# Softmax sums of a decoder layer: the probabilities of two key tiles are added on VectorE before the round with ones, and the order is rewritten

## The chip, the core and the metric

The kernel runs on one core of one Trainium2 chip. The core has five engines that run side by side, each through its own queue in order: TensorE (matmul, PE in the profile; its weight loads are shown apart as PEld), VectorE (DVE), ScalarE (ACT), GpSimd (POOL) and SyncE (SP, which issues the DMAs). They meet only through semaphores. The metric is the device time of one launch in microseconds (us), the median of the runs.

## The reference, cut to what matters

32 sequences of 256 tokens by 256 features go through one decoder layer: layer norm and self-attention with rotary embedding (16 heads of 16 features), layer norm and cross-attention to 77 context tokens (16 heads), and then a graph of six nodes, each of them an attention with 8 heads of 32 features over its own mixes of earlier nodes, with a last layer norm. All of it is float32. The attention of a node is:

```python
q = ew[c, 0] * (nodes[in_q] @ We[eq] + be[eq])
k = ew[c, 1] * (nodes[in_k] @ We[ek] + be[ek])
v = ew[c, 2] * (nodes[in_v] @ We[ev] + be[ev])
...
scores = jnp.einsum('bqhd,bkhd->bhqk', qh, kh) / jnp.sqrt(jnp.asarray(dh, q.dtype))
attn = jax.nn.softmax(scores, axis=-1)
ctx = jnp.einsum('bhqk,bkhd->bqhd', attn, vh).reshape(B, S, d)
...
nodes[c] = act_w[c] * o + q
```

The change concerns the sum under the softmax, over 256 keys, which the kernel keeps as two key tiles of 128.

## The kernel before, in words

A launch is a prologue (weights are loaded and folded, about 128 us), one pass over the pieces marked as running ahead, and a loop of 16 iterations. An iteration carries two sequences, called slot 0 and slot 1, through eight stages: stage 0 is self-attention (SELF), stage 1 cross-attention (CROSS), stages 2 to 7 are the nodes. The slots run interleaved, so that one has matmuls while the other waits for a chain.

The work is cut into pieces, and one text, `ORDER` (lines 134 to 201), lists all pieces of an iteration. Each engine walks through this list and issues those that are its own, in this order; nothing else sets the order. A name such as `PV1.3.0@6` reads: piece PV, slot 1, stage 3, group 0, in PSUM bank 6. A plus marks a piece that works on the next iteration's sequence. What a piece must wait for is worked out from the list as counts of semaphores.

The pieces of one group of four heads (SELF and CROSS have four groups a slot, a node two) are, in order:

- S, SB on TensorE: scores, queries in rows, from a high and a low half (three products); MX on VectorE (line 863): the maximum of each row, two heads an operation; NM on GpSimd (679, 682): the negated maximum, split in two halves.
- MT on TensorE, MR on ScalarE: the maxima are transposed. ST, SX on TensorE: the scores again, keys in rows, less the maximum.
- EX on ScalarE (773): exp of two heads and both key tiles, into `probs`. 
- PV on TensorE (1037 to 1056): first, for each key tile and head, a matmul with a matrix of ones, which sums the probabilities over the keys into the right half of the bank; then the same for the values, into the left half. With two key tiles that is 8 and 8 matmuls, in CROSS with its one tile 4 and 4. Each is 32 columns of the array wide, so that four run side by side.
- RC on ScalarE (783, 785): 1/sum as exp(-ln(sum)); NR on VectorE (874 to 877): a Newton step, and the product with the context. OA and OB on TensorE: the output projection. NE: a node's result is kept.

Other names: LNS and LNN (VectorE, 806 to 819), LNP (GpSimd) are layer norm; TR and TRE transpose its result `n_tok` into `h_t`; Q, K, V are projections, QH, QL, KH, KL the high and low halves of their results; QI, QR, QC, QS and KI, KR, KC, KS are the rotary embedding of SELF, which uses `n_tok` as a buffer as well. FA, FG, FX end a sequence. The profile files nearly all matmuls under line 893, the helper; the tile names tell them apart. A float32 matmul shows as two records: the 8 matmuls with ones of a group are 16 records.

## Time and profile before

| | |
|---|---|
| median of 3 runs | 5447.38 us (5445.13 to 5449.93) |
| the profiled execution: its own time | 5450.77 us |
| the profiled execution: its span | 5449.0 us |
| mean granted TensorE clock, share of full speed | 0.953 |
| one iteration (16 in the loop) | about 329 us |
| TensorE busy, VectorE busy, ScalarE busy | 93%, 51%, 46% of the span |

Busy time is a union: two matmuls side by side count once. In order of time, a row of the profile gives the start and duration of a run of like instructions, how many records it holds, and in brackets how long its engine had been idle before it and what ended that. Because matmuls are pipelined, the shown duration of a run reaches into that of the next; the time that a run takes in the queue is the distance from its start to the next start.

### The profile page before, as it was taken

To read this page: it belongs to the slowest core of one execution; us is meant where nothing else is said; L and a number is where in the kernel's file an instruction comes from. 1 tells how busy PE (TensorE), PEld (TensorE's weight loads), DVE (VectorE), ACT (ScalarE), POOL (GpSimd) and SP (SyncE) were. 2 spreads that over 40 slices of the span, in tenths; PEclk is the share of its full clock that TensorE was granted. 3 is DMA by queue.
4 is the path that set the end of the run, shared out by engine and by line. 5 is a ranking of instruction groups with operands and counts; after the bars stand their busy time and mean duration, and the time that the engine had idled before them with its cause. 6 is when DMAs were issued, how large, how long until landed. Compare 5 with 4: busy or idle time off the path is not lost.

```text
span 5449.0 us, 155972 instructions
## 1 busy us (share of the span) xinstructions
PE 5088.6 (93%) x64256; PEld 3743.1 (69%) x64256; DVE 2799.5 (51%) x5095; ACT 2516.2 (46%) x4784; POOL 656.1 (12%) x1756
## 2 busy tenths in 40 slices
PE   5898998989999898998989999899998989999899
PEld 5576676767767676776767667676776767767676
DVE  2445455454554555455454554555455455554555
ACT  0354554544445444554544444454454444445444
POOL 0101001010110201002010110201002010110201
PEclk8899998999999999998999999899998999999899
DMA  3000000000000000000000000000000000000000
GB/s 124 7 2 10 3 2 11 2 11 2 8 5 2 11 2 10 3 2 11 2 10 3 8 5 2 11 2 10 3 2 11 2 10 3 6 7 2 11 2 8
DMA packets 45096, 46.93 MB, mean 9 GB/s; under 512 B 11969, under 2 KB 44097, under 8 KB 44353
## 3 DMA queue, kind: packets, MB, share of 16 engines
q1 hardware_dynamic: 36480, 28.59, 1.7%
q8 instruction: 549, 8.99, 0.7%
q10 hardware_dynamic: 7872, 7.76, 0.4%
q14 instruction: 195, 1.59, 0.1%
HBM read 27.95 MB, written 8.39 MB: 7 GB/s over the span
## 4 chain that ended last, share of the span: by engine, by line
PE 51%; issue 35%; DVE 5%; POOL 3%; ACT 2%; POOLq 0%; ACTq 0%; DVEq 0%
PE banks L893 50%; DVE row_max L863 3%; PE banks L1010 1%; ACT probs L773 1%; POOL neg_max L679 1%; POOL neg_max L682 1%; POOL inv_std L658 1%; DVE q_parts L835 0%; PE banks L940 0%; DVE rope_s L832 0%; POOL var_eps L655 0%; ACT k_parts L731 0%; DVE k_parts L841 0%; DVE rope_s L828 0%; ACT q_parts L721 0%
## 5 line engine op out<-in xcount | busy, mean ns | idle before, releaser
L863 DVE TENSOR_REDUCE row_max<-banks 128x4 f32<-128x1024 f32 (+1 forms) x1293 | 1327.7, 1070 | 774.2 <-PE banks L893 738.4
L773 ACT ACTIVATE probs<-banks 128x1024 f32<-128x1024 f32 (+1 forms) x1288 | 1139.2, 935 | 598.2 <-PE banks L893 596.7
L893 PE MATMUL banks<-k_parts,q_parts 32*128 32x256 f32 x12472 | 525.2, 299 | 173.0 <-DVE row_max L863 67.2
L893 PEld LDWEIGHTS banks<-k_parts,q_parts 32*128 32x128 f32 x12472 | 423.9, 189 | 325.1 <-issue 219.2
L893 PE MATMUL banks<-node_t,w_n 128*128 128x256 f32 x2560 | 637.4, 391 | 5.5 <-ACT node_t L790 5.5
L893 PE MATMUL banks<-q_parts,k_parts 32*128 32x256 f32 x12384 | 526.9, 302 | 38.2 <-DVE row_max L863 31.9
L893 PEld LDWEIGHTS banks<-q_parts,k_parts 32*128 32x128 f32 x12384 | 423.6, 192 | 200.4 <-issue 128.1
L893 PEld LDWEIGHTS banks<-node_t,w_n 128*128 128x128 f32 x2560 | 462.6, 189 | 123.9 <-issue 39.5
L679 POOL TENSOR_TENSOR neg_max<-row_max,zeros 128x8 fp32r<-128x8 f32 x645 | 143.5, 222 | 3341.1 <-DVE row_max L863 3336.6
L764 ACT ACTIVATE max_rows<-banks 128x256 fp32r<-128x256 f32 x514 | 195.2, 383 | 657.3 <-PE banks L1010 657.2
L783 ACT ACTIVATE context_t<-banks 128x256 f32<-128x256 f32 x514 | 198.1, 385 | 639.3 <-PE banks L893 639.0
L848 DVE SCALAR_TENSOR_TENSOR q_parts<-banks,b_n,q_parts 128x256 fp32r<-128x256 f32 x384 | 171.6, 478 | 579.8 <-ACT q_parts L737 579.8
L893 PE MATMUL banks<-h_t,w_n 128*128 128x256 f32 x1792 | 450.7, 397 | 0.0
L874 DVE TENSOR_TENSOR probs<-banks,context_t 128x256 f32<-128x256 f32 x449 | 189.2, 421 | 498.7 <-ACT context_t L785 496.4
L893 PE MATMUL banks<-probs,ones 128*32 128x256 f32 x6144 | 420.5, 392 | 20.5 <-DVE row_max L863 20.5
L893 PE MATMUL banks<-probs,v_full 128*32 128x256 f32 x6144 | 409.6, 385 | 0.0
L893 PEld LDWEIGHTS banks<-h_t,w_n 128*128 128x128 f32 x1792 | 337.7, 196 | 73.1 <-issue 16.0
L893 PE MATMUL banks<-w_n,node_t 128*128 128x256 f32 x1536 | 370.0, 384 | 0.0
L893 PE MATMUL banks<-context_t,w_n 128*128 128x256 f32 x1280 | 319.7, 384 | 0.0
L893 PEld LDWEIGHTS banks<-w_n,node_t 128*128 128x128 f32 x1536 | 282.0, 190 | 46.2 <-issue 6.6
L893 PEld LDWEIGHTS banks<-probs,v_full 128*32 128x32 f32 x6144 | 202.6, 112 | 138.8 <-issue 10.8
L893 PEld LDWEIGHTS banks<-probs,ones 128*32 128x32 f32 x6144 | 163.7, 110 | 175.3 <-issue 43.7
(126 smaller groups left out, 6343.6 us busy)
## 6 DMA issues: line engine op xcount, KB each, us to landing
x_next<-in_x SPq DMA_DIRECT2D x34, 256.0 KB, 2.7
out_y<-x_tok SPq DMA_DIRECT2D x32, 256.0 KB, 2.1
w_head<-in_wf SPq DMA_DIRECT2D x2, 1536.0 KB, 12.9
c_t<-in_ctx_t SPq DMA_DIRECT2D x34, 77.0 KB, 2.2
w_edge_t<-in_we_t ACTq DMA_DIRECT2D x10, 256.0 KB, 12.0
w_edge_t<-in_we_t SPq DMA_DIRECT2D x10, 256.0 KB, 11.6
w_head<-in_wf ACTq DMA_DIRECT2D x1, 1536.0 KB, 10.0
w_n<-in_we ACTq DMA_DIRECT2D x3, 256.0 KB, 11.5
```

The lines of the kernel that those rows point to most:

```text
L658: done(pool.tensor_tensor(inv_std[s][:, n, :], var_eps[s][:, n, :], minus_half[:, :], ALU.pow), "inverse_std", a)
L679: done(pool.tensor_tensor(parts[:, :, :, 2 * i], negated, zeros[:, :, :], ALU.add), "max_split", (a, "high"))
L682: done(pool.tensor_tensor(parts[:, :, :, 2 * i + 1], negated, parts[:, :, :, 2 * i].bitcast(F32), ALU.subtract), "max_split", (a, "low"))
L764: done(act.activation(max_rows[s][:, a[3], :], bank_of(("MT", s, j, a[3]))[:, 0:T], ACT.Copy), "max_rows_kept", a)
L773: done(act.activation(probs[s][0:rows, g % 2, 2 * p:2 * p + 2, 0:kt, :] .rearrange("p c k t -> p c (k t)"), psum[0:rows, b0:b0 + 2, 0:kt * T],
L783: done(act.activation(ctx_t_sb[s][:, a[3], :], bank[:, T:2 * T], ACT.Ln), "log_taken", a)
L848: done(dve.scalar_tensor_tensor(q_parts[s][:, 1, d, :], bank_of(("Q", s, j))[:, d * T:(d + 1) * T], proj_bias("Q", j, d), q_parts[s][:, 0, ...
L863: done(dve.reduce_max(row_max[s][:, g, 2 * p:2 * p + 2, :].rearrange("p c q -> p (c q)"), psum[:, b0:b0 + 2, :].rearrange("p c (q t) -> p ...
L874: done(dve.tensor_tensor(product, bank[:, T:2 * T], inverse, ALU.mult), "newton_in", (a, "product"))
L893: return nc.tensor.matmul(bank_ap, lhs, rhs, start=start, stop=stop, **kw)
L1010: last = nc.tensor.transpose(bank_of(a)[:, q * P:(q + 1) * P], neg_max[s][:, u, q, :].bitcast(F32), ident[:, :])
```

## The change

VectorE gets a new piece, PA, two for each group of SELF and the nodes (CROSS has one key tile and gets none). PA waits for one EX and adds that EX's two key tiles, two heads in one operation, 512 elements a row. The first pair's result goes to `n_tok` of the slot, the second's to the new `pair_sums`; both wait until the sums of the group before are done (`old_sums`). TensorE's PV keeps the values alone (8 matmuls, in CROSS 4), and a new piece PS holds the round with ones: 4 matmuls, over the added tiles. RC waits for PS. EX, which overwrites `probs`, waits for PV and PA. `n_tok` now stays occupied through the nodes, so that the next sequence's layer norm (LNN0.0, LNN1.0) waits for the last PS of the slot. To make room, the halves of CROSS's keys, `kx_parts`, are moved into `k_parts`. The text of the order is written anew: 942 pieces in place of 838, other banks, and another place where the iteration begins.

```diff
@@ old_scores, began
-    return [last_scores(s, CROSS if j == CROSS else j - 2 if j - 2 >= FFN0 else SELF)]
+    return [last_scores(s, j - 2 if j - 2 >= FFN0 else SELF if j == CROSS else CROSS)]
...
+def old_sums(s, j, g):
+
+    if g:
+        return "PS", s, j, g - 1
+    i = LAST if j == SELF else SELF if j == FFN0 else j - 1
+    return "PS", s, i, last_group(i)
...
@@ ORDER
-PV0.7.0@5 RC0.7.0 NR0.7.0 QL1.7.0 ST0.7.1@0 SX0.7.1 EX0.7.1.1 EX0.7.1.0 +Q0.0@4 +QB0.0 +QI0.0 S1.7.0@0 SB1.7.0
+PV0.7.0@5 PA0.7.0.1 PS0.7.0 EX0.7.1.0 QL1.7.1 QL1.7.0 PA0.7.1.1 PA0.7.1.0 PV0.7.1@7 PS0.7.1 RC0.7.0 RC0.7.1
...
@@ decoder
-        kx_parts = [sb(f"kx_parts{s}", [P, 4, KC, TAIL], F32R) for s in range(SLOTS)]
+        pair_sums = [sb(f"pair_sums{s}", [P, 2, T]) for s in range(SLOTS)]
...
+        def added(s, p):
+
+            return n_tok[s][:, :, :] if p == 0 else pair_sums[s][:, :, :]
...
@@ scalar_step, EX
-                act.wait_ge(sem["context_ready"], reached(at, "context_ready", old_probs(s, j, g)))
+                old = old_probs(s, j, g)
+                act.wait_ge(sem["context_ready"], reached(at, "context_ready", ("PV",) + old))
+                if old[1] == CROSS:
+                    act.wait_ge(sem["sums_ready"], reached(at, "sums_ready", ("PS",) + old))
+                else:
+                    act.wait_ge(sem["tiles_added"], reached(at, "tiles_added", *[("PA",) + old + (i,) for i in range(2)]))
...
@@ vector_step, LNN
+                    dve.wait_ge(sem["sums_ready"], reached(at, "sums_ready", ("PS", s, LAST, last_group(LAST))))
...
+            elif k == "PA":
+                g, p = a[3:]
+                both = probs[s][:, g % 2, 2 * p:2 * p + 2, :, :]
+                dve.wait_ge(sem["exp_done"], reached(at, "exp_done", ("EX", s, j, g, p)))
+                dve.wait_ge(sem["sums_ready"], reached(at, "sums_ready", old_sums(s, j, g)))
+                done(dve.tensor_tensor(added(s, p), both[:, :, 0, :], both[:, :, 1, :], ALU.add), "tiles_added", a)
...
@@ tensor_step, PV
-                for what in range(2):
-                    for q in range(kt):
-                        for c in range(4):
...
-                            last = matmul(bank_of(a)[ROWS * c:ROWS * (c + 1), (1 - what) * T:(2 - what) * T],
-                                          lhs, probs[s][0:m, g % 2, c, q, :],
-                                          what == 0 and q == 0 and e == 0, q == kt - 1, skip_group_check=True)
+                for q in range(kt):
+                    for c in range(4):
+                        lhs = (v_full[s][:, q, P * x + ROWS * c:P * x + ROWS * (c + 1)] if j >= FFN0
+                               else v_half[s][0:m, q, 4 * x + c, 16 * e:16 * e + 32])
+                        last = matmul(bank_of(a)[ROWS * c:ROWS * (c + 1), 0:T], lhs, probs[s][0:m, g % 2, c, q, :],
+                                      q == 0 and e == 0, q == kt - 1, skip_group_check=True)
                 done(last, "context_ready", a)
+            elif k == "PS":
...
+                for c in range(4):
+                    lhs = ones[0:m, :] if j >= FFN0 else half_ones[0:m, 16 * e:16 * e + 32]
+                    rhs = probs[s][0:m, g % 2, c, 0, :] if j == CROSS else added(s, c // 2)[:, c % 2, :]
+                    last = matmul(bank_of(a)[ROWS * c:ROWS * (c + 1), T:2 * T], lhs, rhs, False, True,
+                                  skip_group_check=True)
+                done(last, "sums_ready", a)
```

How the instructions now stand is shown at three places. In these rows the number behind a name is the slot; the REGISTER_ALU rows compute the value for a wait. The first place is TensorE in node stage 4, around the second group of slot 0 (PV0.4.1). Before:

```order
L893 MATMUL banks<-k_parts1,q_parts1 128x256 x24
L893 MATMUL banks<-probs0,ones 32x256 x8
L893 MATMUL banks<-probs0,v_full0 32x256 x8
L893 MATMUL banks<-node_t0,w_n 128x256 x4
L925 REGISTER_ALU
L893 MATMUL banks<-q_parts1,k_parts1 128x256 x24
```

After, at the same place:

```order
L929 MATMUL banks<-k_parts1,q_parts1 128x256 x24
L929 MATMUL banks<-probs0,v_full0 32x256 x8
L961 REGISTER_ALU
L929 MATMUL banks<-n_tok0,ones 32x256 x2
L929 MATMUL banks<-pair_sums0,ones 32x256 x2
L961 REGISTER_ALU
L929 MATMUL banks<-node_t0,w_n 128x256 x4
L961 REGISTER_ALU
L929 MATMUL banks<-q_parts1,k_parts1 128x256 x24
```

The values come first, and the four matmuls with ones follow directly, behind a wait of their own. The second place is TensorE at the end of slot 0's last node, where the next sequence's SELF begins. Before:

```order
L893 MATMUL banks<-max_rows0,select 128x256 x8
L893 MATMUL banks<-h_t0,w_qkv 128x256 x4
L925 REGISTER_ALU x2
L893 MATMUL banks<-k_parts1,q_parts1 128x256 x24
L893 MATMUL banks<-n_tok0,rot 128x512
L893 MATMUL banks<-probs0,ones 32x256 x8
L893 MATMUL banks<-probs0,v_full0 32x256 x8
```

After, from the same SX0.7.1 on:

```order
L929 MATMUL banks<-max_rows0,select 128x256 x8
L961 REGISTER_ALU
L929 MATMUL banks<-probs0,v_full0 32x256 x8
L961 REGISTER_ALU
L929 MATMUL banks<-n_tok0,ones 32x256 x2
L929 MATMUL banks<-pair_sums0,ones 32x256 x2
L929 MATMUL banks<-probs0,v_full0 32x256 x8
L961 REGISTER_ALU
L929 MATMUL banks<-n_tok0,ones 32x256 x2
L929 MATMUL banks<-pair_sums0,ones 32x256 x2
L929 MATMUL banks<-k_parts1,q_parts1 128x256 x16
```

Before, the next sequence's query projection (h_t0, w_qkv) stood between SX0.7.1 and the values of that group; its TR0.0 stood in stage 5 and V0.0 in stage 6. Now both PV of stage 7 stand directly behind SX0.7.1, and TR0.0, Q0.0 and V0.0 come after them. The third place is VectorE there, from the last row maxima of slot 0's stage 7 on. Before:

```order
L863 TENSOR_REDUCE row_max0<-banks 128x4 x2
L870 REGISTER_ALU
L874 TENSOR_TENSOR probs0<-banks,context_t0 128x256
L875 TENSOR_TENSOR context_t0<-banks,context_t0 128x256
L876 REGISTER_ALU
L877 SCALAR_TENSOR_TENSOR context_t0<-probs0,context_t0 128x256
L847 REGISTER_ALU
L848 SCALAR_TENSOR_TENSOR q_parts1<-banks,b_n,q_parts1 128x256
```

After:

```order
L893 TENSOR_REDUCE row_max0<-banks 128x4 x2
L912 REGISTER_ALU
L914 TENSOR_TENSOR n_tok0<-probs0 128x512
L912 REGISTER_ALU
L914 TENSOR_TENSOR pair_sums0<-probs0 128x512
L877 REGISTER_ALU
L878 SCALAR_TENSOR_TENSOR q_parts1<-banks,b_n,q_parts1 128x256 x2
L912 REGISTER_ALU
L914 TENSOR_TENSOR pair_sums0<-probs0 128x512
L912 REGISTER_ALU
L914 TENSOR_TENSOR n_tok0<-probs0 128x512
```

The four additions of stage 7 stand between the row maxima and the layer norm of the next sequence (two TENSOR_SCALAR into `n_tok0`), which follows them; before, that norm stood at the start of stage 2.

## Rows read from the trace of the kernel before

**Rows 1.** The page: the engines' busy time, share and instructions.

```profile
PE 5088.6 (93%) x64256; PEld 3743.1 (69%) x64256; DVE 2799.5 (51%) x5095; ACT 2516.2 (46%) x4784; POOL 656.1 (12%) x1756
```

**Rows 2.** Stretches: us, busy time per engine (instructions), TensorE clock, DMA share, GB/s.

```profile
2487.00:2816.00 329.00, 311.19 (x3970) 228.12 (x3969) 172.28 (x312) 156.47 (x299) 41.55 (x110) 0.96 0.02 6
2565.00:2758.00 193.00, 190.48 (x2363) 142.48 (x2361) 91.50 (x150) 98.21 (x189) 10.35 (x46) 1.00 0.01 2
2758.00:2790.00 32.00, 28.20 (x363) 19.47 (x360) 25.52 (x39) 12.78 (x23) 8.77 (x18) 0.95 0.03 10
2790.00:2820.00 30.00, 28.02 (x327) 19.54 (x325) 17.11 (x41) 16.17 (x29) 10.96 (x12) 1.00 0.09 28
2820.00:2838.00 18.00, 10.57 (x196) 9.72 (x196) 13.37 (x19) 0.04 (x1) 3.73 (x13) 0.67 0.02 5
2838.00:2894.00 56.00, 53.99 (x728) 36.86 (x726) 24.89 (x68) 28.79 (x57) 7.49 (x22) 0.89 0.02 5
```

**Rows 3.** Who waited for whom, whole span: us in total, times, longest.

```profile
PE banks L893 <- DVE row_max L863: 140.0, 135, 3.0
...
PE banks L893 <- issue: 48.3, 16, 4.4
```

**Rows 4.** Groups by line and shape: busy us, mean ns, idle before and releaser.

```profile
L863 DVE TENSOR_REDUCE row_max<-banks 128x4 f32<-128x1024 f32 x1037 | 1218.8, 1217 | 741.9 <-PE banks L893 711.1 <-issue 28.1 <-PEq L1072 0.5
...
L893 PE MATMUL banks<-probs,ones 128*32 128x256 f32 x6144 | 420.5, 392 | 20.5 <-DVE row_max L863 20.5
...
L893 PE MATMUL banks<-probs,half_ones 128*32 128x256 f32 x2112 | 143.2, 389 | 12.3 <-ACT probs L773 12.3
```

**Rows 5.** TensorE in order of time: start, us, what it ran.

```profile
2526.21 0.62 PE L893 MATMUL banks<-probs,half_ones 77*32 77x256 f32 x8
2526.65 0.61 PE L893 MATMUL banks<-probs,v_half 77*32 77x256 f32 x8
...
2599.86 1.07 PE L893 MATMUL banks<-probs,ones 128*32 128x256 f32 x16
2600.75 1.05 PE L893 MATMUL banks<-probs,v_full 128*32 128x256 f32 x16
2601.72 1.99 PE L893 MATMUL banks<-h_t,w_n 128*128 128x256 f32 x8
```

**Rows 6.** Groups by shape: VectorE's additions 512 wide.

```profile
L832 DVE TENSOR_TENSOR rope_s<-rope_s,rope_c 128x512 f32<-128x512 f32 x68 | 49.2, 723 | 2.3
...
L890 DVE TENSOR_TENSOR x_tok<-node_t,x_tok 128x512 f32<-128x512 f32 x32 | 22.0, 687 | 44.0 <-POOL node_t L689 44.0
```

**Rows 7.** VectorE and GpSimd in order of time, two places where they meet.

```profile
2787.60 0.68 DVE L890 TENSOR_TENSOR x_tok<-node_t,x_tok 128x512 f32<-128x512 f32 x1
...
2787.76 0.58 POOL L679 TENSOR_TENSOR neg_max<-row_max,zeros 128x8 fp32r<-128x8 f32 x1 [3.57 <-DVE row_max L863]
...
2788.59 0.21 POOL L679 TENSOR_TENSOR neg_max<-row_max,zeros 128x8 fp32r<-128x8 f32 x1
...
2813.62 1.38 POOL L671 TENSOR_TENSOR rope_c<-n_tok,cos_t 128x512 f32<-128x512 f32 x1 [0.71 <-ACT n_tok L707]
...
2814.10 1.46 DVE L835 TENSOR_TENSOR q_parts<-rope_s,q_parts 128x512 fp32r<-128x512 f32 x1 [0.21 <-ACT q_parts L721]
...
2766.28 0.68 DVE L835 TENSOR_TENSOR q_parts<-rope_s,q_parts 128x512 fp32r<-128x512 f32 x1
```

**Rows 8.** TensorE, then ScalarE, in order of time around the start of SELF.

```profile
2757.70 0.40 PE L893 MATMUL banks<-max_rows,select 32*128 32x256 f32 x8
...
2785.47 1.93 PE L893 MATMUL banks<-probs,ones 128*32 128x256 f32 x16 [1.28 <-DVE row_max L863]
...
2758.15 1.94 ACT L773 ACTIVATE probs<-banks 128x1024 f32<-128x1024 f32 x2 [0.30 <-PE banks L893]
```

**Rows 9.** TensorE, then VectorE, at the end of the loop's body.

```profile
2830.01 0.80 PE L893 MATMUL banks<-k_parts,q_parts 32*128 32x256 f32 x8 [2.70 <-issue]
...
2828.93 1.22 DVE L863 TENSOR_REDUCE row_max<-banks 128x4 f32<-128x1024 f32 x1 [1.73 <-issue]
```

More of the change, by code:

```diff
@@ L99, in began @@
     k, s, j = key[:3]
-    if k == "PV" and place(*key[2:])[1] == 1:
-        return "PV", s, j, key[3] - 1
+    if k == "PS" or (k == "PV" and place(*key[2:])[1] == 1):
+        return "PV", s, j, key[3] - place(*key[2:])[1]
     if k in ("SB", "SX"):
@@ new lines @@
+KH1.1 ST0.1.2@4 SX0.1.2 EX0.1.2.0 EX0.1.2.1 LNS1.1 V1.1@3 PV0.1.1 PS0.1.1 RC0.1.0 ST0.1.3@4 LNP1.1 LNN1.1
+SX0.1.3 EX0.1.3.1 EX0.1.3.0 PV0.1.2@0 TR1.1@2 PS0.1.2 NR0.1.0 KL1.1 TRE1.1 PV0.1.3 PS0.1.3 RC0.1.1 NR0.1.1
+Q1.1@2 QB1.1 OB0.1.0@1 QH1.1.0 QH1.1.1 QL1.1.0 QL1.1.1 OB0.1.1 XB1.1 XA0.1 S1.1.0@4 SB1.1.0 MX1.1.0.0 MX1.1.0.1
+VE1.1 S1.1.1@0 SB1.1.1 MX1.1.1.0 NM1.1.0 MX1.1.1.1 S1.1.2@4 SB1.1.2 S1.1.3@0 MX1.1.2.0 MX1.1.2.1 NM1.1.1 SB1.1.3
+LNS0.2 MT1.1.0@6 MR1.1.0 ST1.1.0@4 LNP0.2 SX1.1.0 EX1.1.0.0 EX1.1.0.1 MX1.1.3.1 MX1.1.3.0 ST1.1.1@0 LNN0.2
@@ L623, in key_parts @@
                 return k_parts[s], 2 * (j % 2)
-            return (kx_parts if j == CROSS else k_parts)[s], 0
+            return k_parts[s], 0
         def proj_bias(k, j, d):
```

174 lines of the change are left out of this document (91 added, 83 removed).

## The prediction, made before the changed kernel ran

> **What bounds the kernel now.** I read the page first. TensorE is busy for 93% of the span, VectorE for 51% [rows 1], so less matmul work should shorten the launch wherever TensorE is really full, and VectorE has room on average. An average hides stages, so next I cut one iteration, 329 us long, into stretches by the windows [rows 2]. The reader is to see two kinds. From 2565 to 2758, most of the node stages, TensorE is busy for 190.48 of 193 us at the full clock, and VectorE for 91.50: here the queue of TensorE is the time. From 2758 to 2838, the end of stage 7 and SELF, it is otherwise: TensorE has 28.20 of 32 us, 28.02 of 30 and 10.57 of 18, while VectorE has 25.52, 17.11 and 13.37. The remaining 56 us, the exponents of slot 1's SELF, both CROSS and the start of stage 2, are nearly full again (53.99) at a clock of 0.89. The waits say who is late in the thin part: TensorE waited 140.0 us in the launch for row maxima, and 48.3 us in 16 waits that nothing in the profile explains [rows 3]; the 16 are the end of the loop's body, 2.70 us at a time [rows 9]. Last I took prices, from the groups by shape and from the order of time.
>
> **What is removed.** A run of 16 records with ones starts at 2599.86 and the values after it at 2600.75: 0.89 us in the queue at full clock [rows 5]. Busy time gives more (420.5 us over 6144 records, 0.068 us a record or 1.09 us for 16 [rows 4]), since a run's shown end overlaps the next run; I take the start distance, for that is what the queue gets back. Half of the run goes, 8 records. That a run of 8 really costs half is shown by CROSS, whose 8 records with ones take 0.44 us from start to start (2526.21 to 2526.65) [rows 5]. So one group saves 0.445 us, at most 0.55 by busy time. There are 6144/16 = 384 groups in the nodes and 2112/16 = 132 in SELF [rows 4], together 516: 516 x 0.445 = 230 us. At half clock a group saves twice as much: a few SELF groups run so, which I leave in the margin. Nothing is saved in CROSS, whose PS is the old round in another place. The additional boundary between PV and PS I take at nothing, because the boundary between ones and values exists today.
>
> **What is added.** Each of the 516 groups gets two additions on VectorE, 128x512, both inputs in SBUF. The trace has this form: 687 and 723 ns in the mean [rows 6]. 1032 x 0.69 = 712 us of VectorE work, which takes it from 2799.5 to some 3510 us, two thirds of the new span. In the node stretch VectorE goes from 91.5 of 193 us to about 91.5 + 42 x 0.69 = 120 (21 groups end there), of some 184: still covered, if the pieces lie well. They do at the first place of the order: PV stands between the last EX and PS. An EX of two heads takes 0.97 us (two in 1.94 [rows 8]); the first pair's addition runs beside the second EX, the second pair's (0.69) beside the values' 0.97 us (2600.75 to 2601.72 [rows 5]). So a PS waits for nothing as long as VectorE is free when EX ends. What stands in front of an addition can be a pair of row maxima, 2 x 1.217 us [rows 4]. Behind a late PS the whole of TensorE's queue is held, the other slot too. I charge no such wait in the node stretch, and keep one addition, 0.69 us, as the upper bound for a group, 0 as the lower.
>
> **What moves, and what it costs.** First, stage 7 of slot 0. The new order puts both PV directly behind SX0.7.1. The exponents take 1.94 us and start about when SX ends (SX starts at 2757.70 and lasts 0.40, EX runs 2758.15 to 2760.09 [rows 8]). In that time TensorE has PV0.7.0 and PS0.7.0, 0.97 + 0.445 = 1.42 us: about 0.6 to 0.8 us idle, 16 x 0.8 = 13 us. Before, a projection stood there.
>
> Second, the stretch 2758 to 2790. VectorE is busy for 25.52 of 32 us and TensorE waits there for row maxima, 1.28 us at 2785.47 alone [rows 2, 8]. To VectorE come eight additions (groups 0.7.0, 0.7.1, 1.7.0, 1.7.1: 5.5 us) and the layer norm LNN0.0 (two operations of about 0.4 us): 31.8 us. The 6.5 us that VectorE idles today are chain waits; if half of them stay, the stretch is 31.8 + 3.3 = 35 us. It also takes over TR0.0 and V0.0 from the node stages, some 2.5 us of matmuls that leave there, so today's 32 has to be compared as 34.5. It grows by 0.5 where the saving of its four groups (1.8) would have shortened it: 2.3 us lost per iteration, 37 us in all. Bounds: 0, if the idle time takes everything, and 5 us per iteration (80), if all idle time stays and the additions come on top.
>
> Third, the loop's end. Today it falls among the row maxima of slot 1's SELF: TensorE idles 2.70 us and VectorE 1.73 [rows 9], and VectorE bounds that stretch. Now it falls between V0.1 and K0.1, where slot 1's rotary chain runs. It frees the row maxima and lengthens the other place. I take 0, between -2.7 and +2.7 us an iteration (43 us either way). The CROSS keys now wait for SELF's last ST, since they share `k_parts`; the queries of CROSS come out of the whole end of SELF and are later still: nothing.
>
> **The meeting of VectorE and GpSimd.** The trace shows one more cost. L890, with both inputs in SBUF, ran 2787.60 to 2788.28, and the negation NM that started at 2787.76 took 0.58 us, until 2788.34; the one at 2788.59 took 0.21. The other way round, the subtraction L835 took 1.46 us beside GpSimd's rope_c, and 0.68 at 2766.28 [rows 7]. Row maxima, which read PSUM, cause nothing of the kind. The added PA is of the form of L890. By the new order five of the 40 NMs of an iteration have a PA as the next VectorE instruction behind their maxima, ten have one within two. NM opens the chain to MT, MR and SX. The price lies between 5 x 0.37 = 1.9 us an iteration (30 us) and 10 x 0.69 (110 us), if all of it fell on the path. I take 0, since MT stands well behind NM in the nodes, and keep 0 to 110.
>
> The Trainium skill (SBUF — State Buffer, "Who interferes with whom") says that a VectorE instruction with two SBUF inputs contends with a GpSimd instruction that reads SBUF, and that whoever issues first holds the other for its whole length. By that rule, the trace agrees: 0.58 in place of 0.21. The rule would price the ten meetings at the full addition each, the upper end above, and it speaks against this change.
>
> **The sum.** Against the execution profiled: 5450.8 - 230 + 13 + 37 = 5271 us. That execution is 3.4 us above the median of the runs (5447.4), so I expect a median of 5267, 3.3% less.
>
> **Rivals.**
> - *The additions come late* (PS waits in the nodes). For: VectorE takes its work in order, and some PA stand behind row maxima or Newton steps, which wait for ScalarE. Against: 91.5 of 193 us, and PV as a cover. 0.2 us on each of 512 loop groups is 102 us: 5370.
> - *The meeting with GpSimd decides.* As above, up to 110 us: 5330 to 5377. For: the rows at 2787; against: TensorE's waits for NM are hardly seen today.
> - *More comes back.* The loop's end is covered and the idle time of SELF swallows the additions: 43 + 37 us more, 5187. For: TensorE has 10.57 of 18 us there at a clock of 0.67, so a shorter stall also gives clock back. The granted clock fell behind the idle stretches: 1.00 in the nodes, 0.67 in 2820 to 2838 [rows 2]. Against: VectorE bounds that place and gets more to do.
> - *Slower.* One mechanism: every PS stands behind an addition that starts only when the values have ended, because VectorE's queue is held by a chain in front of it. It breaks even at a wait of 230 - 50 = 180 us over 512 groups, 0.35 us. At one whole addition, 0.69, it costs 353 us: 5267 + 353 = 5620; at the 0.5 us that I think the most likely size of it, 5520. For: Newton steps and row maxima wait in VectorE's queue for other engines, and an addition behind them waits too. Against: VectorE's idle time in the nodes, 100 of 193 us today, would have to miss all the additions.
> - *The rounds don't get cheaper*: four matmuls as a piece of their own cost as much as eight (a fixed cost). The CROSS rows, 0.44 against 0.89, speak against it. About 5450.
>
> **Chances.** Forecast 0.58, its own range 5210 to 5330. Late additions 0.13. GpSimd 0.07. More back 0.12. Slower 0.07. No cheaper rounds 0.03. The range for eight in ten: down to 5190, which takes most of the third rival, and up to 5375, which takes the second and most of the first; outside are slower, no change, and the tails. A measurement of this kernel can tell 0.2% (11 us) from no change: faster 0.58 + 0.13 + 0.07 + 0.12 = 0.90, the same 0.03, slower 0.07.
>
> **What would show it.** Records with ones: 3072 in place of 6144, their busy time about 210 us; TensorE busy about 4810 to 4860; VectorE about 3500, with the additions at 0.69 us. In the node stages PV then PS with 0.97 and 0.45 us between starts and no idle time ahead of PS, and an iteration of about 318 us. A wait of TensorE on line 914 with a total above 50 us means the first rival; NMs of 0.5 us and more in numbers, with TensorE idle before MT, the second; a stretch around SELF shorter than today's the third. If TensorE's busy time falls by 230 and the span by less than 150, my stage costs are too small; if busy time itself doesn't fall, the price of a round was wrong.

## The result, and the profile of the changed kernel

The changed kernel takes 5374.24 us (median of 4 runs, 5366.34 to 5380.52) where the kernel before takes 5448.66 on the same chip (4 runs, 5445.13 to 5451.14): a ratio of 0.9863, 95% interval 0.9845 to 0.9881. That is 74 us or 1.4% faster. The prediction said 5267: the direction is right, and the gain is 74 us where 182 were forecast. One run of one experiment (e12, 7265.31 us at a granted clock of 0.671, where its other three have 0.893 to 0.898) is left out of its figures.

The page of the changed kernel, its row of busy times (engine, us, share of the span, instructions), compares with [rows 1]. Its span is 5364.5:

```profile
PE 4867.7 (91%) x60002; PEld 3588.7 (67%) x60002; DVE 3470.4 (65%) x6103; ACT 2508.1 (47%) x4767; POOL 684.6 (13%) x1751
```

TensorE's busy time fell by 221 us (5088.6 to 4867.7), and the span by only 84.5 (5449.0 to 5364.5). So 136 us of what was taken from TensorE came back as idle time of TensorE. The view of waits (who waited for whom, us in total, times, longest) says for whom:

```profile
PE banks L929 <- DVE row_max L893: 151.3, 203, 2.5
PE banks L929 <- ACT probs L802: 81.2, 145, 1.5
...
PE banks L929 <- issue: 43.0, 15, 3.2
PE banks L929 <- DVE q_parts L878: 31.0, 48, 0.9
...
PE banks L929 <- DVE n_tok L914: 24.6, 33, 1.0
...
PE banks L929 <- DVE pair_sums L914: 10.0, 16, 0.6
```

Two rows of the same view of the kernel before, which [rows 3] does not have:

```profile
PE banks L893 <- ACT probs L773: 25.5, 66, 1.5
...
PE banks L893 <- DVE q_parts L848: 3.7, 2, 1.9
```

Against [rows 3] the row maxima grew little in total (140.0 to 151.3) but from 135 waits to 203, and the loop's end (issue) lost 5. The largest growth is at the exponentials (25.5 to 81.2, 56 of the 136), then at the two tiles of sums (34.6 together, new) and the low parts of the queries (3.7 to 31.0); SELF's transposed input h_t (11.7) is nearly all new. No single wait is long: it is a thin growth over many.

The groups by shape for the two halves of the additions, and for the new round in the nodes, to be read against [rows 4] and [rows 6] (busy us, mean ns, idle before):

```profile
L914 DVE TENSOR_TENSOR n_tok<-probs 128x512 f32<-128x512 f32 x516 | 373.7, 724 | 275.7 <-ACT probs L802 176.2 <-PE banks L929 94.6
L914 DVE TENSOR_TENSOR pair_sums<-probs 128x512 f32<-128x512 f32 x516 | 365.2, 708 | 414.1 <-ACT probs L802 239.9 <-PE banks L929 174.2
...
L929 PE MATMUL banks<-n_tok,ones 128*32 128x256 f32 x1536 | 232.9, 382 | 17.5 <-DVE pair_sums L914 10.0 <-DVE n_tok L914 7.5
```

The records with ones in the nodes are 3072, as foreseen: 1536 over `n_tok`, and as many over `pair_sums`, whose 232.9 us lie beside them. The right-hand numbers of the additions matter more: VectorE stood 690 us ahead of additions, 416 of them for an exponential and 269 for TensorE, whose earlier round frees the tile.

The order of time on TensorE, four places (start, us, what ran, idle before and its releaser):

```profile
2540.83 1.07 PE L929 MATMUL banks<-probs,v_full 128*32 128x256 f32 x16
2541.72 0.39 PE L929 MATMUL banks<-n_tok,ones 128*32 128x256 f32 x2
...
2542.26 1.99 PE L929 MATMUL banks<-h_t,w_n 128*128 128x256 f32 x8
...
2574.03 0.98 PE L929 MATMUL banks<-k_parts,q_parts 32*128 32x256 f32 x24 [0.26 <-DVE q_parts L878]
...
2575.89 1.07 PE L929 MATMUL banks<-probs,v_full 128*32 128x256 f32 x16 [0.47 <-ACT probs L802]
...
2716.74 1.07 PE L929 MATMUL banks<-probs,v_full 128*32 128x256 f32 x16 [0.68 <-ACT probs L802]
...
2774.57 1.15 PE L929 MATMUL banks<-c_t,w_x 128*128 128x77 f32 x8 [2.58 <-issue]
```

Where the queue is full, values and sums take 0.89 and 0.54 from start to start, 1.43 against 1.86 before [rows 5]: 0.43 a group, as priced. At 2574 and 2575 stand small waits of a kind that the node stages hardly had. At 2716.74 is the wait foreseen for slot 0's PV in stage 7 (0.68, forecast 0.6 to 0.8), and at 2774.57 the loop's end (2.58 against 2.70 [rows 9]).

The node stretch by the windows, the counterpart of 2565 to 2758 in [rows 2]:

```profile
2529.00:2714.00 185.00, 177.72 (x2141) 133.76 (x2143) 118.73 (x193) 94.92 (x179) 12.55 (x48) 1.00 0.01 2
```

TensorE idles 7.3 us in it, where it idled 2.5. From step to same step (the `h_t,w_n` matmuls in stage 2 to the end of SX0.7.1) it is 185.4 us. Before it was 193.5. Twenty groups at 0.43 are 8.6 less; 3.3 less for matmuls that moved out of the stretch (a transpose, SELF's values, the keys of CROSS); and 1.86 less for the group of PV0.7.0, which stood ahead of SX0.7.1 and now stands behind it. That makes 179.7. So the node stages lose 5.7 us an iteration, where the prediction had nothing. Only 0.6 of it is a wait for sums (before PS0.5.0). Three waits for the low parts of queries (0.26, 0.77 and 0.91) make 1.9, and the rest are short waits for exponentials and row maxima. The whole iteration, from loop end to loop end, is 324.0 us in the mean (327.7 before).

### The profile page after: what moved, and what is told of

The parts are those of the page before. It is cut to its first block, busy times and chain, and to the rows that moved or that the text cites. A ratio compares the mean times of both kernels' runs of the same rounds, so it can differ in the third digit from the quotient of the medians.

```text
span 5364.5 us, 151607 instructions
## 1 busy us (share of the span) xinstructions
PE 4867.7 (91%) x60002; PEld 3588.7 (67%) x60002; DVE 3470.4 (65%) x6103; ACT 2508.1 (47%) x4767; POOL 684.6 (13%) x1751
## 4 chain that ended last, share of the span: by engine, by line
PE 75%; issue 10%; DVE 8%; ACT 3%; POOL 0%; DVEq 0%; ACTq 0%; POOLq 0%
PE banks L929 72%; DVE row_max L893 5%; PE banks L1046 2%; ACT probs L802 1%; PE banks L976 1%; DVE n_tok L914 1%; ACT q_parts L761 1%; DVE q_parts L878 1%; ACT k_parts L755 1%; DVE k_parts L871 0%; DVE pair_sums L914 0%; ACT k_parts L768 0%; DVE k_parts L885 0%; DVE rope_s L862 0%; ACT max_rows L788 0%
## 5 line engine op out<-in xcount | busy, mean ns | idle before, releaser
L929 PE MATMUL banks<-k_parts,q_parts 32*128 32x256 f32 (+1 forms) x15456 | 661.0, 307 | 187.3 <-DVE row_max L893 90.4
L929 PEld LDWEIGHTS banks<-k_parts,q_parts 32*128 32x128 f32 x15456 | 545.5, 201 | 357.9 <-issue 184.2
L929 PE MATMUL banks<-q_parts,k_parts 32*128 32x256 f32 (+1 forms) x13920 | 607.5, 303 | 89.9 <-DVE row_max L893 59.9
L929 PEld LDWEIGHTS banks<-q_parts,k_parts 32*128 32x128 f32 (+1 forms) x13920 | 471.9, 188 | 285.2 <-issue 143.4
L914 DVE TENSOR_TENSOR pair_sums<-probs 128x512 f32<-128x512 f32 x516 | 365.2, 708 | 414.1 <-ACT probs L802 239.9
L929 PE MATMUL banks<-node_t,w_n 128*128 128x256 f32 x2560 | 625.5, 388 | 0.0
L703 POOL TENSOR_TENSOR neg_max<-row_max,zeros 128x8 fp32r<-128x8 f32 x644 | 156.8, 243 | 3352.3 <-DVE row_max L893 3350.0
L914 DVE TENSOR_TENSOR n_tok<-probs 128x512 f32<-128x512 f32 x516 | 373.7, 724 | 275.7 <-ACT probs L802 176.2
L929 PE MATMUL banks<-probs,v_full 128*32 128x256 f32 x6144 | 410.8, 385 | 31.5 <-ACT probs L802 29.7
L929 PEld LDWEIGHTS banks<-probs,v_full 128*32 128x32 f32 x6144 | 161.9, 109 | 179.6 <-ACT probs L802 48.3
## 6 DMA issues: line engine op xcount, KB each, us to landing
w_head<-in_wf SPq DMA_DIRECT2D x2, 1536.0 KB, 12.8
```

What stands on the lines that cost most here:

```text
L703: done(pool.tensor_tensor(parts[:, :, :, 2 * i], negated, zeros[:, :, :], ALU.add), "max_split", (a, "high"))
L914: done(dve.tensor_tensor(added(s, p), both[:, :, 0, :], both[:, :, 1, :], ALU.add), "tiles_added", a)
L929: return nc.tensor.matmul(bank_ap, lhs, rhs, start=start, stop=stop, **kw)
```

## The experiments

Fifteen kernels were run. The kernel before ran beside them on the same chip each time, with a median between 5446.2 and 5449.7. Three terms had to be told apart: the halved round, the new order, the additions.

### The three terms, one by one

**e2_order_only.** The new order, the old rounds, no additions.

```
             elif k == "PS":
...
-                wait_for(..., ("tiles_added", ("PA", s, j, g, 0)), ("tiles_added", ("PA", s, j, g, 1)))
-                for c in range(4): ... rhs = added(s, c // 2)[:, c % 2, :]
+                for q in range(key_tiles(j)):
+                    for c in range(4): ... rhs = probs[s][0:m, g % 2, c, q, :]
```

> The new order with the old computation: no additions, PS is the old round of eight matmuls with ones over both key tiles, behind PV. Theory A: the order itself costs nothing, about 5450 us, like the kernel before. Theory B: the order costs what was missing, 5530 to 5560 us. In between, the two share.

Measured: 5493.59 (5486.15 to 5503.87), ratio 1.0089 [1.0073, 1.0106]. The new order by itself costs 48 us.

**e4_half_round_old_order.** The order of before, half a round over a constant tile, no additions.

```
-                    for q in range(kt):
+                    for q in range(1 if what == 0 else kt):
...
-                                          lhs, probs[s][0:m, g % 2, c, q, :],
+                                          lhs, flat[0:m, :] if what == 0 and j != CROSS else probs[s][0:m, g % 2, c, q, :],
```

> The kernel before, in its own order, with four in place of eight matmuls with ones in SELF and the nodes, over a constant tile (sums not those of the reference) and no additions: what the halved round is worth by itself. Both theories: 5449 - 230 = 5219 us if TensorE's queue is the time wherever the round stands. If the saving is swallowed by waits for VectorE and ScalarE even without additions (theory C): 5280 to 5330.

Measured: 5303.74 (5294.85 to 5314.24), ratio 0.9741 [0.9723, 0.9758]. With neither a new order nor additions, the halved round gives 142 us and not 230. This is the largest part of the miss: 88 us.

**e1_tiny_adds.** The changed kernel with each addition cut to two elements.

```
-  done(dve.tensor_tensor(added(s, p), both[:, :, 0, :], both[:, :, 1, :], ALU.add), "tiles_added", a)
+  done(dve.tensor_tensor(added(s, p)[:, 0, 0:2], both[:, 0, 0, 0:2], both[:, 0, 1, 0:2], ALU.add), "tiles_added", a)
```

> The changed kernel with the same pieces, waits and order, but each addition on VectorE is cut to two elements a row; the matmuls with ones of SELF and the nodes read a constant tile instead of the added one, so the softmax sums are not those of the reference. Theory A (the additions' time on VectorE took the missing 96 us): 5270 us or less, since the 230 us of matmul work are saved and nothing of length is added. Theory B (the rewritten order leaves less cover on TensorE, whatever VectorE adds): about 5340 to 5370, hardly below the changed kernel.

Measured: 5356.94 (5352.21 to 5360.52), ratio 0.9832 [0.9815, 0.9848]: 17 us under the changed kernel. The two intervals just touch, so the 17 is a rough figure. It also makes the halved round worth 137 us in the new order (5493.6 to 5356.9), much as in the old.

**e3_one_input.** The additions replaced by a reduction of the same length with one input in SBUF.

```
-  done(dve.tensor_tensor(added(s, p), both[:, :, 0, :], both[:, :, 1, :], ALU.add), "tiles_added", a)
+  done(dve.tensor_reduce(added(s, p)[:, :, 0:T // 2], both[:, :, 0, :].rearrange("p c (t r) -> p c t r", r=2),
+                         AX_X, ALU.add), "tiles_added", a)
```

> The changed kernel with each addition of two SBUF inputs replaced by a reduction that reads 512 elements a row of one SBUF tile, some 0.6 to 0.7 us as well, so that VectorE is as busy but has one SBUF input; the matmuls with ones read a constant tile (sums not those of the reference). If the meeting of VectorE and GpSimd costs (NM 25 us longer in sum): about 5345 us or less and NM back at 0.21 us. If VectorE's plain time is what costs: 5370, the same as the changed kernel.

Measured: 5345.19 (5338.13 to 5354.04), ratio 0.9813 [0.9797, 0.9829], 29 us under the changed kernel, though VectorE is as busy (3432 us). The groups of the row-maximum negation NM on GpSimd, first of the changed kernel, then of this one:

```profile
L703 POOL TENSOR_TENSOR neg_max<-row_max,zeros 128x8 fp32r<-128x8 f32 x644 | 156.8, 243 | 3352.3 <-DVE row_max L893 3350.0
L706 POOL TENSOR_TENSOR neg_max<-row_max,neg_max 128x8 fp32r<-128x8 f32 x644 | 148.3, 230 | 50.4
```

```profile
L705 POOL TENSOR_TENSOR neg_max<-row_max,zeros 128x8 fp32r<-128x8 f32 x644 | 139.7, 217 | 3371.0 <-DVE row_max L894 3368.7
L708 POOL TENSOR_TENSOR neg_max<-row_max,neg_max 128x8 fp32r<-128x8 f32 x644 | 139.1, 216 | 50.5
```

With two inputs in SBUF the NMs take 243 and 230 ns, with one 217 and 216, as in the new order without additions (e2): GpSimd's 26.3 us are the meeting. VectorE's own operations are shorter too, 682 and 681 ns in place of 708 and 724, 35 us in all, and TensorE's wait for `n_tok` falls from 24.6 to 5.4. The 29 us are the meeting's upper end here. This kernel and e1 also differ from the changed one in that the round reads a constant tile and an exponential waits for the round before it, so the meeting's share is not separated further. And e1 is not a clean zero: with 478 us less of VectorE work than e3 it took 12 us more, and its TensorE was busy 29 us longer (4897.4 against 4868.3, at a clock of 0.955 against 0.959). Why is not known.

The sum of the parts, 5446 - 142 + 48 + 17, is 5369, beside 5374 measured. Since the 17 was itself taken from 5374, this tests one thing: that the halved round and the new order add up (5352, beside 5357 in e1). That the additions add to the other terms in any order is not shown, and e8 below refutes it.

### Why the halved round gives 142 and not 230

**e5_half_self and e6_half_nodes** do e4's edit in the 132 groups of SELF alone, and in the 384 of the nodes alone; the added lines are that of the first, then that of the second.

```
-                    for q in range(1 if what == 0 else kt):
+                    for q in range(1 if what == 0 and j == SELF else kt):
+                    for q in range(1 if what == 0 and j >= FFN0 else kt):
```

> The order of before and its eight matmuls with ones, except in the 132 groups of SELF, where four over a constant tile stand in for the sums (the denominators of SELF are left out of the computation; no additions). Theory A, the saved time is kept only where TensorE is the last to arrive: SELF is paced by ScalarE's exponentials (0.97 each, two a group, against a group of TensorE) and by the row maxima, so next to nothing comes back, 5446 to 5430. Theory B, a fixed part of every group's saving is lost (142 of 230 everywhere): -36, so 5410. My prediction's price, 132 x 0.445 = 59: 5387.

> The order of before, four matmuls with ones over a constant tile in the 384 groups of the node stages, eight elsewhere (the denominators of the node stages are left out; no additions). Theory A: 142 less what SELF gives, so -125 to -142, 5304 to 5321. Theory B: 384/516 x 142 = -106, so 5340. My prediction's price, 384 x 0.445 = 171: 5275.

Measured: SELF alone 5446.86 (5442.85 to 5450.14), ratio 0.9995 [0.9986, 1.0005]: nothing. The nodes alone 5345.01 (5342.68 to 5350.33), ratio 0.9812 [0.9796, 0.9828]: 104 us of the 171. The two do not add up to e4's 142. The page and the waits, first of SELF alone, then of the nodes alone, then of both (e4):

```profile
PE 5037.7 (93%) x63200; PEld 3706.1 (68%) x63200; DVE 2803.5 (52%) x5096; ACT 2512.7 (46%) x4784; POOL 656.1 (12%) x1756
```

```profile
PE banks L895 <- ACT probs L775: 60.1, 114, 1.5
PE banks L895 <- issue: 58.5, 16, 4.6
```

```profile
PE banks L895 <- DVE row_max L865: 169.7, 169, 3.0
PE banks L895 <- issue: 68.3, 32, 4.8
...
PE banks L895 <- ACT probs L775: 31.7, 66, 1.5
```

```profile
PE banks L895 <- DVE row_max L865: 164.9, 172, 3.0
PE banks L895 <- ACT probs L775: 59.7, 112, 1.5
PE banks L895 <- issue: 48.3, 32, 4.4
```

In SELF alone TensorE's busy time falls by 50.9 us (5088.6 to 5037.7), and 34.6 of it return as waits for exponentials (25.5 in the kernel before) and 10.2 at the loop's end (48.3 before): the span falls by 6. In the nodes TensorE's busy time falls by 165.0, and 29.7 return at the row maxima, 20.0 at the loop's end, 7.0 at NM (2.9 before, 9.9 now) and 6.2 at exponentials. In both together the loop's end is back at 48.3, which is most of why both give more than the sum. SELF went as theory A had it. The nodes' 104 is the number of theory B (106) and not of A (125 or more), but the 20 us at the loop's end make the difference, so the two runs do not decide between them. In e4 TensorE's busy time falls by 216 (5088.6 to 4872.4), and 66 of it return: 34.2 at exponentials, 24.9 at row maxima, 7.0 at NM.

**e13_light_before and e14_light_half_round** test that directly. In both, row maxima and exponentials do half of the columns; the second has four matmuls with ones in place of eight.

```
-                                    [:, :, 0:TC if j == CROSS else T], AX_X, negate=True), "max_taken", a)
+                                    [:, :, 0:TC if j == CROSS else T // 2], AX_X, negate=True), "max_taken", a)
...
-                                    psum[0:rows, b0:b0 + 2, 0:kt * T],
+                                    psum[0:rows, b0:b0 + 2, 0:kt * T // 2],
```

> The kernel before with the row maxima taken over, and the exponentials done for, half of the columns (the other half of the maxima's input is left out, and the second key tile's probabilities are zeros). All steps, waits and TensorE's work stay. TensorE waits 140 for maxima and 25.5 for exponentials in the kernel before, so at most some 165 comes off: 5290 to 5400.

> The same with four instead of eight matmuls with ones in each of the 516 groups, over a constant tile (compare with the full-length pair: 142 between them). If VectorE's and ScalarE's long operations set the pace where the saving was lost, the difference to the kernel before with the same light operations is 200 to 230. If TensorE itself gives back only 0.275 a group, it stays at 140 to 150.

Measured: 5275.09 (5272.24 to 5283.40) and 5054.20 (5052.80 to 5056.73). The difference is 221 us, where the same edit gave 142 beside full-length operations. The page's first row of the two, and their waits for maxima:

```profile
PE 5038.1 (95%) x64256; PEld 3730.9 (71%) x64256; DVE 2273.5 (43%) x5097; ACT 2034.6 (39%) x4784; POOL 652.1 (12%) x1756
```

```profile
PE 4810.1 (95%) x60128; PEld 3593.4 (71%) x60128; DVE 2256.6 (45%) x5098; ACT 2037.3 (40%) x4784; POOL 657.6 (13%) x1756
```

```profile
PE banks L894 <- DVE row_max L864: 44.3, 64, 1.5
...
PE banks L894 <- DVE k_parts L842: 20.1, 12, 1.7
...
PE banks L894 <- DVE q_parts L849: 7.4, 4, 1.9
```

```profile
PE banks L896 <- DVE row_max L866: 43.9, 63, 1.5
```

TensorE's busy time falls by 228 and its waits for maxima stay at 44: nearly all of the price of 0.445 a group (221 of 230) reaches the end as soon as the other two engines are quicker. The theory that a fixed part of the price is not real falls. Which of the two engines takes back how much was not tried, since both were shortened together. The light kernel before is itself 175 us faster than the kernel before, below the 5290 to 5400 expected: besides shorter waits, TensorE's busy time fell by 50.5 at a higher granted clock (0.960 against 0.953).

### Where the order's 48 us are

**e15_light_order** is e2 with the same short maxima and exponentials.

```
+                                    [:, :, 0:TC if j == CROSS else T // 2], AX_X, negate=True), "max_taken", a)
+                                    psum[0:rows, b0:b0 + 2, 0:kt * T // 2],
```

> The new order with eight matmuls with ones and no additions, with the same light maxima and exponentials (with full ones it stood 48 over the kernel before). If its 48 is waits for these two, it vanishes: within 15 of the light kernel before. If it is in the move of steps past others (keys of CROSS, transposes at the loop's end, the low parts of the queries), most of it stays: 30 to 60 over.

Measured: 5311.97 (5311.66 to 5312.43), 37 over the light kernel before. Its waits:

```profile
PE banks L919 <- DVE row_max L889: 51.1, 97, 1.4
...
PE banks L919 <- DVE q_parts L874: 44.2, 48, 1.2
PE banks L919 <- DVE k_parts L867: 29.9, 33, 1.7
...
PE banks L966 <- DVE n_tok L845: 12.8, 16, 9.0
```

The row maxima make 7 of it. The low parts of the queries make 37 (7.4 to 44.2), the keys' 18 (20.1 to 29.9 and 8.4), SELF's late layer norm and transpose stand for 12.8 and 11.7; the loop's end gives 21 back (49.5 to 28.6). All three waits for the low parts of queries in an iteration lie in the node stages. So most of the 48 are moves of chains: layer norm, transpose, queries and keys stand closer to their readers. Which of these moves the additions force, and which merely came with the new text, was not tried. With full-length operations (e2) the exponentials are among the waits too: 47.6 against 25.5.

### What the additions need

**e7_double_adds.** The changed kernel with every addition done twice, first into a spare tile.

```
+                dve.tensor_tensor(again[:, :, :], both[:, :, 0, :], both[:, :, 1, :], ALU.add)
                 done(dve.tensor_tensor(added(s, p), both[:, :, 0, :], both[:, :, 1, :], ALU.add), "tiles_added", a)
```

> The changed kernel with every addition done twice, first into a spare tile, then as now: VectorE's busy time grows by about 739 to 4210 of some 5400. If the additions lie in VectorE's idle time and cost 17 in all (5374 against 5357 with them cut), a second set should cost some tens: 5390 to 5430. If the first set already uses up the slack ahead of the rounds with ones, each of the 516 rounds comes up to 0.7 to 1.4 later and the time grows by 200 to 500.

Measured: 5744.27 (5736.49 to 5748.27), ratio 1.0538 [1.0520, 1.0555]: 370 us more. The first set cost 17 to 29, the second 370. (Each addition here also waits for the one before it to end.) Its page and waits:

```profile
PE 5027.7 (87%) x60002; PEld 3627.0 (63%) x60002; DVE 4104.8 (71%) x7135; ACT 2512.6 (44%) x4767; POOL 707.3 (12%) x1751
```

```profile
PE banks L933 <- DVE n_tok L918: 139.0, 123, 2.9
...
PE banks L933 <- DVE pair_sums L918: 82.2, 115, 1.7
```

TensorE waits 221 us for sums, and its own work takes 160 longer at a lower granted clock (mean 0.941 against 0.961).

**e11_self_not_added.** The changed kernel with SELF's rounds as before: all PA of stage 0 leave the list, and `PLAIN` is SELF and CROSS.

```
-+SX0.0.1 +EX0.0.1.1 +EX0.0.1.0 +PA0.0.0.1 FA1 +PA0.0.0.0
++SX0.0.1 +EX0.0.1.1 +EX0.0.1.0 FA1
...
-                if j == CROSS:
+                if j in PLAIN:
...
-                for c in range(4):
+                for q in range(key_tiles(j) if j in PLAIN else 1):
```

> The changed kernel without the additions of SELF: its 132 groups have eight matmuls with ones on the probabilities as before (264 additions, 187 of VectorE's time, gone; 528 matmuls, some 57 of TensorE's, back). Halving SELF's rounds alone gave nothing in the old order (5447), and 38 more when the nodes' were halved. If ScalarE's exponentials and the maxima pace SELF here too, this is as fast as the changed kernel or faster, 5350 to 5375. If TensorE's 57 are on the path, 5390 to 5430.

Measured: 5375.41 (5374.29 to 5380.24), ratio 0.9868 [0.9851, 0.9884], the same as the changed kernel: SELF's 132 groups, a quarter of the change, bring nothing. TensorE is busy for 58 us more (4925.3), and 47 us of waits are gone: the loop's end has 29.1 in place of 43.0, the sums 13.3 in place of 34.6, the exponentials 69.3 in place of 81.2.

**e8_adds_in_before_order.** The whole change in the old order.

```
-... EX1.2.1.0 ... PV1.2.1@6 RC1.2.1 NM0.3.0 ...
+... EX1.2.1.0 ... PA1.2.1.1 PA1.2.1.0 PV1.2.1@6 PS1.2.1 RC1.2.1 NM0.3.0 ...
```

> The whole change, real additions and halved rounds, in the order of before: the additions stand directly ahead of the PV step of their group, the round with ones directly behind it, and only the keys of CROSS are moved (one buffer for the keys of all stages, as in the changed kernel); slot 0 has a tile of its own for the first sum, so that layer norm, transpose and values of SELF stay where they were. If the parts add up (halved round -142, additions +17, the order's own +48 not paid): 5321. If the additions need the new order, because in the old one VectorE's queue has row maxima and low parts in their way: 5374 or more, with new waits of TensorE on the two tiles of sums far over the 35 that the changed kernel shows.

Measured: 6180.70 (6174.11 to 6195.12), ratio 1.1350 [1.1331, 1.1369]. The expectation of 5321 is off by 860: the additions do not add to the other terms; here, unlike in the new order, they are dear. The profiled run's span is 6176.9 at a granted clock of 0.898. TensorE's waits (`first_sums` is slot 0's own tile for the first pair), and then VectorE's:

```profile
PE banks L929 <- DVE pair_sums L914: 356.2, 189, 3.8
PE banks L929 <- DVE first_sums L914: 178.3, 80, 3.3
...
PE banks L929 <- DVE n_tok L914: 44.7, 16, 2.8
```

```profile
DVE q_parts L878 <- ACT q_parts L761: 369.6, 128, 8.1
```

TensorE stands 579 us for sums, while VectorE idles 44% of the span (35% in the changed kernel). VectorE is not short of time. It stands ahead of steps that wait for another engine, up to 8.1 us ahead of a query's low part, and the additions stand behind those steps.

**e10_tiny_in_before_order** is e8 with additions of two elements (e1's edit). **e12_adds_early_in_before_order** is e8 with each PA directly behind its EX in the list. **e9_sums_at_once** puts the rule of e8 (PA, PA, PV, PS) into the new order. Its edit is of the kind shown, all through the list: five PS move up to their PV, and 29 of the 64 additions change places with VectorE's other steps, 26 of them to stand later by one to five steps.

```
-PV1.0.0@2 NM0.1.2 PA1.0.0.1 PA1.0.0.0 PS1.0.0 ST1.0.2@4 ...
+PA1.0.0.1 PA1.0.0.0 PV1.0.0@2 PS1.0.0 NM0.1.2 ST1.0.2@4 ...
```

> The kernel of 6181 (order of before, additions ahead of PV, halved rounds behind it) with each addition cut to two elements; the rounds with ones read a constant tile (the denominators are left out of the computation). All its waits are kept, VectorE's work of some 730 is gone. If VectorE's time for the additions costs the 877 (6181 against the sum of parts of 5304), it falls to 5304 to 5350. If it is the standing and waiting of VectorE for the exponentials, with maxima and low parts queued behind, it stays over 5700.

> The kernel of 6181 with each addition moved up VectorE's queue, directly behind its exponential in the list (or behind the earlier round that frees its tile): 60 of 64 with no other step of VectorE between, where 6181 had up to 5. If late additions are what cost the time, most of it comes back, 5350 to 5500. If VectorE standing in line for ScalarE costs the same as what it holds up (row maxima, for which TensorE waits), it stays over 5700.

> The changed kernel with the two additions of every group directly ahead of its PV step in the list and its round of ones directly behind it (the rule by which they were put into the old order, where the kernel took 6181). In the list of the changed kernel 35 of 40 rounds stand directly behind their PV already, and VectorE's other steps between an exponential and its addition are at most 4, so this is a small edit. If the old order is slow because of this rule, this one is far slower than 5374 too, 5600 or more. If it is the rest of the old order (what VectorE has queued between the exponentials and the additions), it stays near: 5380 to 5480.

Measured: e10 5688.32 (5684.67 to 5701.95), ratio 1.0449 [1.0431, 1.0466]; e12 6302.22 (6289.10 to 6313.36), ratio 1.1577 [1.1554, 1.1600]; e9 5759.97 (5742.82 to 5768.35), ratio 1.0566 [1.0543, 1.0589]. TensorE's waits in e10, in e12, and in e9:

```profile
PE banks L930 <- DVE pair_sums L915: 192.3, 112, 2.7
...
PE banks L930 <- DVE first_sums L915: 77.1, 66, 2.3
```

```profile
PE banks L929 <- DVE context_t L907: 303.2, 142, 4.1
```

```profile
PE banks L929 <- DVE n_tok L914: 223.5, 107, 2.7
...
PE banks L929 <- DVE pair_sums L914: 86.5, 65, 1.6
```

With additions of two elements the old order still takes 385 us more than with none (5304 to 5688). That is neither of e10's two expectations; it lies near the second. TensorE waits 297 us for sums in it (192.3, 77.1 and 27.6 at `n_tok`). Most of the 385 is therefore the mere standing in line, though e10 also has the keys of CROSS moved, and its waits for keys are 21 longer than e4's (48.0 against 26.9). The additions' own time makes the other 492. The Trainium skill (PSUM — Partial Sum Buffer, "Engine vs sequencer instructions") calls VectorE's queue strict first in, first out. The rows agree: an addition of two elements still keeps TensorE waiting up to 2.7 us, for what stands ahead of it.

Moving the additions up (e12) frees the sums (36.7 and 30.3 us of waits in place of 356.2 and 178.3) and delays what they now hold up, above all the Newton step (context_t, 303.2).

I expected 5380 to 5480 for e9 and was wrong by 280 or more; it costs 386 over the changed kernel. The trace says where. This is TensorE at PS0.2.1, then VectorE at the same time:

```profile
2725.77 1.07 PE L929 MATMUL banks<-probs,v_full 128*32 128x256 f32 x16
2729.51 0.64 PE L929 MATMUL banks<-n_tok,ones 128*32 128x256 f32 x2 [2.67 <-DVE n_tok L914]
```

```profile
2725.89 2.35 DVE L893 TENSOR_REDUCE row_max<-banks 128x4 f32<-128x1024 f32 x2 [3.37 <-PE banks L929]
2728.16 0.68 DVE L914 TENSOR_TENSOR pair_sums<-probs 128x512 f32<-128x512 f32 x1
2728.76 0.69 DVE L914 TENSOR_TENSOR n_tok<-probs 128x512 f32<-128x512 f32 x1
```

In the changed kernel the two additions stand ahead of slot 1's row maxima. Here they stand behind them. VectorE idles 3.37 us until TensorE has made the scores for these maxima, does the maxima (2.35), and only then the additions, while TensorE stands 2.67 us at the round that needs them. In this iteration TensorE waits for sums eleven times, 18.8 us in all. Nine of these waits (16.2 us) are at rounds whose additions were moved back past maxima or other steps, and one (1.54, at PS0.6.0) at a round that was itself moved up; the other four moved rounds wait for nothing.

## Why the prediction was wrong, step by step

**The removed rounds, 230 us: mis-sized, this is the main failure.** The price of a group is right: 0.43 from start to start, a TensorE busy time lower by 221 (by 216 in e4, at the same granted clock of 0.953 as before), and 221 us of gain once maxima and exponentials are short. What was wrong is the step from that price to the launch: 516 x 0.445, as if TensorE's queue were the time at every group. It was measured at 142 us (137 in the new order), 88 less than forecast. The prediction itself had found TensorE not full in SELF and charged SELF's 132 groups in full all the same, 59 of the 230. They give 2 us in e5: of the 50.9 that TensorE saves there, 34.6 return at ScalarE's exponentials and 10.2 at the loop's end. The node stages lose at the row maxima and NM as TensorE gets ahead. A stretch in which TensorE is busy for 190.48 of 193 us [rows 2] has 2.5 us of idle time, but that doesn't say how far behind the next engine is. The last line of the prediction foresaw the sign of it: a busy time down by 230 and a span down by less than 150 mean that costs elsewhere were too small.

**The moved steps, 50 us: right in sum by luck, wrong in place.** The new order costs 48, measured without any addition, while the forecast's 37 of the 50 were worked out from the load of eight additions. The stall at slot 0's PV in stage 7 came as worked out (0.68). But the larger part lies at the low parts of queries, in the node stages, and then at the keys and at SELF's layer norm and transpose. The prediction looked for the order's cost at three places (stage 7, the stretch from 2758, the loop's end) and charged the rest nothing. No run singled out VectorE's load around 2758. "I charge no such wait in the node stretch", said of waits for sums, nearly held: 0.6 us an iteration. But the stretch lost 5.7 us an iteration, mostly to other waits.

**The loop's end, 0: right in sum.** 43.0 us in 15 waits against 48.3 in 16. Two things cancel in it: the order alone brings it to 28.6 (e2), and with the halved round it is back at 45.6 (e1) and 43.0. Why the halved round lengthens it is not known.

**The additions, 0: nearly right, by luck of the order.** They cost 17 to 29. TensorE's waits on sums are 34.6, under the 50 named as the sign of the first rival. But the reason given, VectorE's 100 idle us of 193, was a bad one: in e8 VectorE idles more and TensorE waits 579 us. The mechanism of the "slower" rival (an addition behind a chain) is real: e8 lies 877 us over the same order with halved rounds and no additions (e4). The new order avoids it and costs 48 itself.

**GpSimd and VectorE, 0 within 0 to 110: the mechanism is there, with a small price.** NMs are at 243 and 230 ns where they have 217 and 216 without the meeting, and the launch pays at most 29 us.

**Rounds no cheaper, and more back:** the first is refuted by a round of 0.54 us from start to start where it was 0.89, the second by the span. The range's upper end, 5375, held the 5366 of the profiled run and, barely, the median.

Together: 88 us too much for the rounds, 17 too little for the additions, 2 too much for the moved steps. That is 103 of the 107 us between 5267 and 5374.

## What to carry to other kernels

Before pricing work taken off the busiest engine, find how far behind the next ones are: shorten *their* operations in a copy and see whether the same saving changes. Here 0.445 us a group was worth 0.275 beside full-length maxima and exponentials, and 0.43 beside short ones. An engine that is 50% idle need not have room for an operation in the middle of a chain: what stands ahead of it in its queue decides, so an order written for the old work has to be rewritten before the new work is judged. Single edits (work halved, order alone, additions cut) say more than any argument over shares, but a sum of them holds for the path on which it was measured: in the old order additions and all that e8 moves with them cost 877 us.

## What the runs showed of the hardware

- A stalled TensorE also ran at a lower granted clock. With nearly the same matmuls its busy time was 4867.7 us at a mean granted clock of 0.961, 5027.7 at 0.941 (e7) and 5215.8 at 0.898 (e8): 348 of e8's 806 us over the changed kernel are longer busy time. The ratio of the clocks accounts for all of that in e8 (an estimate: 4867.7 x 0.961 / 0.898 = 5209) and for about 103 of the 160 us in e7. The total of idle time alone does not set the clock: the kernel before, with 360 us idle against 497, had 0.953 against the changed kernel's 0.961.
- TensorE's wait at the loop's end differs between kernels whose step there is the same: 2.6 to 3.5 us in the kernel before, 2.4 to 3.4 with every round halved, but 3.4 to 4.8 with the nodes' alone, in all 15 turns. In the new order it is 1.5 to 2.2 with full rounds (e2) and 2.5 to 3.2 in the changed kernel. That is up to 20 us of a launch, and its cause was not found.
- VectorE additions with two inputs in SBUF lengthened GpSimd's small operations by 26 and 14 ns in the mean (217 to 243, 216 to 230), a one-input reduction of the same length not at all.
